# All of x ahead of the rank-16 tables, and unit 0's split weights parked in HBM for unit 8, in a one-core stack of four conditioned residual layers

## The reference, cut to what matters

```python
x = x + einsum('bct,bcd->bdt', x, w0[ia]) + bias[ia][:, :, None]       # layer 0, 64x64 per sample
gate = x @ Wg + (x @ Ag[ia]) @ Bg[ia]                                  # layer 1, 512 -> 2048, rank 16
up   = x @ Wu + (x @ Au[ia]) @ Bu[ia]
h    = silu(gate) * up
x = x + h @ Wd + (h @ Ad[ia]) @ Bd[ia]                                 # 2048 -> 512
x = x + x @ W.T + scal[ib] * (x @ A[ib].T) @ Bm[ib].T                  # layer 2, 512 -> 512, rank 16
x = x + einsum('bct,bcd->bdt', x, w3[ic])                              # layer 3, 64x64 per sample
```

## Time and profile before

| | |
|---|---|
| median of 3 runs | 761.57 us (761.23 to 762.88) |
| the profiled execution | 756.74 us |
| its span, first to last instruction | 754.9 us |
| PE busy | 719.9 us |
| VectorE busy | 583.3 us |
| ScalarE busy | 286.8 us |
| GpSimd busy | 261.7 us |
| mean granted clock of PE | 0.993 |

### The profile page before, as it was taken

One profiled execution on the slowest core, in us unless ns is written; L12 is line 12 of the kernel. 1 busy time (PEld: TensorE's weight loads), 2 busy tenths in 40 slices (PEclk: granted clock), 3 DMA queues, 4 the chain that ended last, 5 costly groups with the idle time before them and its releaser, 6 DMA issues.

```text
span 754.9 us, 10625 instructions
## 1 busy us (share of the span) xinstructions
PE 719.9 (95%) x3666; PEld 610.6 (81%) x3666; DVE 583.3 (77%) x979; ACT 286.8 (38%) x502; POOL 261.7 (35%) x489
## 2 busy tenths in 40 slices
PE   8598889999999999998899999999999999899997
PEld 7576678888888888877778888888888888788885
DVE  5966868797878788789988879797978796864542
ACT  1445423333424243343353433333424242434444
POOL 3933641415233232342237161616253331222100
PEclk9799999999999999999999999999999999999999
DMA  6486321213212121413712222322222043201112
GB/s 155 141 140 201 116 74 35 99 45 103 82 58 84 56 84 56 84 29 112 246 61 94 68 93 70 105 65 88 81 66 85 29 131 93 83 29 51 63 56 83
DMA packets 80725, 66.02 MB, mean 87 GB/s; under 512 B 42912, under 2 KB 65440, under 8 KB 80672
## 3 DMA queue, kind: packets, MB, share of 16 engines
q1 hardware_dynamic: 73056, 45.92, 20.7%
q0 software_dynamic: 7296, 19.41, 8.4%
q10 hardware_dynamic: 320, 0.02, 0.0%
HBM read 56.94 MB, written 8.39 MB: 87 GB/s over the span
## 4 chain that ended last, share of the span: by engine, by line
PE 79%; DVE 9%; issue 6%; DMA 2%; ACT 2%; POOL 1%; SPq 0%; POOLq 0%; DVEq 0%; ACTq 0%
PE bank L1394 34%; PE bank L1494 21%; PE bank L1402 7%; PE bank L1634 5%; PE bank L1504 4%; PE bank L1623 2%; PE bank L1651 2%; DMA BR<-in_L_cond_Bu_dram,boffs 1%; PE bank L1610 1%; PE bank L1640 1%; PE bank L1347 1%; DMA adsel<-in_L_cond_weights_dram 1%; DVE hid L1040 1%; DVE hs L1046 1%; PE bank L1371 1%
## 5 line engine op out<-in xcount | busy, mean ns | idle before, releaser
L1394 PE MATMUL bank<-XC,WC 128*128 128x512 f32 x1344 | 331.8, 393 | 10.6 <-DVE tmp L1014 3.7
L1394 PEld LDWEIGHTS bank<-XC,WC 128*128 128x128 f32 x1344 | 244.0, 189 | 58.2 <-DVE tmp L1014 4.1
L1494 PE MATMUL bank<-hs,wds 128*128 128x512 f32 x768 | 186.3, 391 | 8.0 <-DVE wds L999 4.1
L1494 PEld LDWEIGHTS bank<-hs,wds 128*128 128x128 f32 x768 | 141.8, 188 | 37.2 <-DVE wds L999 4.6
L421 POOL DMA_INDIRECT BR<-in_L_cond_Bu_dram,boffs x64 | 70.7, 1104 | 258.6 <-DVE BL L993 244.0
L421 POOL DMA_INDIRECT BR<-in_L_cond_Bg_dram,boffs x64 | 76.1, 1189 | 92.7 <-DVE BL L993 77.0
L638 ACT ACTIVATE hs<-hid 128x512 fp32r<-128x512 f32 x64 | 40.3, 630 | 168.1 <-DVE hid L1040 112.9
L1057 DVE TENSOR_TENSOR XA<-bank,XA 128x512 f32<-128x512 f32 x128 | 86.4, 686 | 18.4 <-PE bank L1494 14.8
L632 ACT ACTIVATE hid<-hid 128x512 f32<-128x512 f32 x48 | 30.4, 633 | 152.1 <-issue 60.4
L1402 PEld LDWEIGHTS bank<-UT,BL 128*128 128x128 f32 x512 | 76.4, 189 | 10.8 <-issue 2.1
L1402 PE MATMUL bank<-UT,BL 128*128 128x256 f32 x512 | 81.8, 282 | 1.6 <-DVE hid L1037 1.3
(11 more groups left out here) (164 smaller groups left out, 809.5 us busy)
## 6 DMA issues: line engine op xcount, KB each, us to landing
RW<-in_L_cond_Wg_dram SPq DMA_DIRECT2D x16, 512.0 KB
RW<-in_L_cond_Wu_dram SPq DMA_DIRECT2D x16, 512.0 KB
RD<-in_L_cond_Wd_dram SPq DMA_DIRECT2D x16, 512.0 KB
out_dram<-XB SPq DMA_DIRECT2D x16, 256.0 KB, 2.1
XB<-in_x_dram SPq DMA_DIRECT2D x8, 256.0 KB, 7.3
x1park<-XB SPq DMA_DIRECT2D x8, 256.0 KB
x2park<-XA SPq DMA_DIRECT2D x8, 256.0 KB, 2.7
XA<-x1park SPq DMA_DIRECT2D x4, 512.0 KB
```

Of the source, the lines that this page charges most:

```text
L1394: last = nc.tensor.matmul(psum[:, :], WC[:, t, left, a, k, :], XC[:, right, b, k, :], start=(first and k == 0 and n == 0), stop=(k == 1 an ...
L1494: last = nc.tensor.matmul(psD[j % 2][:, :], by_feature(wds[:, f, a, :])[:, j % KT, :], hs[:, f, b, j // KT * 512:(j // KT + 1) * 512], sta ...
```

## The change

1. **x ahead of A.** SyncE's queue loads all first-half pairs and four of the second half before Ag and Au; the other four follow before the table of indices and Wu. GpSimd places the `w0` tiles of pairs 8 to 13 before it selects A, and those of 14 and 15 after. Layer 0 uses three PSUM banks instead of four, so that each `layer0(p)` waits for the copy of p - 3; the bank that is set free holds the second half of `adapters_in`'s result (`u_bank`).
2. **New orders up to unit 1.** All four engines get another list for the start: on PE pairs 8 and 9 go ahead of the first product, 10 and 11 behind it, and `adapters_in` comes after the second and the third product. `us` moves to the part of `WC` where unit 0's up sums will lie, `raw_high(U, 0)` no longer waits for the selects, `sums_high(U, 0)` does. In unit 1 `sum_u3` and `sum_half22` go ahead of `sums_low(U)`, and in units 1 and 9 the `evict`s of tiles 2 to 4 go ahead of an `hs_low`.
3. **Unit 0's split weights kept for unit 8.** `wpark` in HBM takes the finished `WC` of gate and up after unit 0's splits (`weights_out`, 128 x 14,336 bytes each), and unit 1's `raw_high` waits for these stores. At the change of halves they come back (`weights_back`, and `sums_back` for the part of up that `us` covers until the last select). `combine`, `raw_high`, `raw_low`, `sums_high` and `sums_low` of unit 8 are gone for both matrices, and so are the loads of Wg and Wu for unit 8.
4. **New order at the change of halves.** The sums T2 and T1 of the second half are made in units 3 and 4, into `w0second` and `udp`, instead of in unit 7 in place in `XB`. `wd_high` and `wd_low` of units 7 and 15 move up between the last `evict`s, and `xc_low(1, T3)` moves from the end of unit 7's up window to behind the last `hs_low`. The stores of the second half's x1 move behind unit 0's weight stores and the load of unit 2's Wg.

```diff
+    wpark = nc.dram_tensor("wpark", (2, P, 7 * 2 * 2 * P), f32).ap()
...
-            return (psD[0], psD[1], psR[0], psR[1])[p % 4]
+            return (psD[0], psD[1], psR[0])[p % 3]
+        def u_bank(h, m):
+            return (psE, (psR[1], psC)[h])[m % 2]
...
-        us = [wcu[:, t * 1024:(t + 1) * 1024].rearrange("p (a t) -> p a t", a=2) for t in range(2)]
+        us = [wcu[:, 1536 + t * 1024:1536 + (t + 1) * 1024].rearrange("p (a t) -> p a t", a=2) for t in range(2)]
...
-                  {B11: XB11, B21: XB21, B22: XB22, T1: XB12, T2: XB11, T3: XB12, T4: XB21}]
+                  {B11: XB11, B21: XB21, B22: XB22, T1: udp[:, :].rearrange("p (k t) -> p k t", k=2),
+                   T2: w0second[:, :, :].rearrange("p a d -> p (a d)").rearrange("p (k t) -> p k t", k=2),
+                   T3: XB12, T4: XB21}]
...
+        def made(unit):
+            return unit + 1 - (unit >= UNITS)
...
+                def weights_out(t):
...
+                    sp.wait_ge(s_wl[t], 1)
+                    sp.dma_start(wpark[t, :, :], WC[:, t, :, :, :, :].rearrange("p s a k f -> p (s a k f)").bitcast(f32)).then_inc(s_wout[t], 16)
...
+                def weights_back(t):
+                    sp.wait_ge(s_wout[t], 16)
+                    wct = WC[:, t, :, :, :, :].rearrange("p s a k f -> p (s a k f)").bitcast(f32)
+                    if t == G:
+                        sp.wait_ge(s_prod, 8 * nG(0, UNITS - 1) + 8)
+                        sp.dma_start(wct, wpark[t, :, :]).then_inc(s_wback[t], 16)
+                    else:
+                        sp.wait_ge(s_prod, 8 * nP(0, UNITS - 1) + 8)
+                        sp.dma_start(wct[:, 0:1536], wpark[t, :, 0:1536]).then_inc(s_wback[t], 16)
+                def sums_back():
+                    sp.wait_ge(s_sel, 4 * HALVES)
+                    wct = WC[:, U, :, :, :, :].rearrange("p s a k f -> p (s a k f)").bitcast(f32)
+                    sp.dma_start(wct[:, 1536:], wpark[U, :, 1536:]).then_inc(s_wsback, 16)
...
-                for p in range(3, 6):
+                for p in range(3, HP):
                     load_x(p)
+                for p in range(HP, HP + XIN):
+                    load_xin(p)
                 load_a(0)
-                load_x(6)
-                load_x(7)
-                for p in range(HP, HP + XIN):
+                for p in range(HP + XIN, PAIRS):
                     load_xin(p)
                 load_idx(2, idx_c)
                 load_u(0)
                 load_g(1)
-                load_xin(HP + 4)
-                load_xin(HP + 5)
...
-                        load_xin(HP + 6)
-                    if n == 3:
-                        load_xin(HP + 7)
+                weights_out(G)
                 load_d(0)
-                for p in range(HP, PAIRS):
-                    park_x1(p)
                 load_u(1)
+                weights_out(U)
                 for unit in range(ALL):
                     turn = unit == UNITS - 1
                     if unit and unit != UNITS:
@@ -347,16 +376,21 @@
                         load_u(unit + 1)
                     if turn:
                         load_a(1)
-                        load_u(unit + 1)
+                        weights_back(G)
+                        weights_back(U)
                         park_x2()
                         load_d(unit + 1)
-                    if unit + 2 < ALL:
+                    if unit + 2 < ALL and unit + 2 != UNITS:
                         load_g(unit + 2)
+                    if unit == 0:
+                        for p in range(HP, PAIRS):
+                            park_x1(p)
                     if turn:
+                        sums_back()
                         x1_back()
-                sp.wait_ge(s_wl[G], ALL)
-                sp.wait_ge(s_wl[U], ALL)
+                sp.wait_ge(s_wl[G], made(ALL - 1))
...
-                    select_a(0, q, cols)
-                for g in range(2, 4):
-                    late = adapters(8 * g, 8)
-                    for p in range(4 * g, 4 * g + 4):
-                        place_w0(p, late[2 * (p - 4 * g):2 * (p - 4 * g) + 2])
+                late = adapters(16, 8)
+                for p in range(HP, HP + 4):
+                    place_w0(p, late[2 * (p - HP):2 * (p - HP) + 2])
+                late += adapters(24, 8)
+                for p in range(HP + 4, PAIRS):
+                    if p == PAIRS - 2:
+                        for q in range(HQ):
+                            select_a(0, q, cols)
+                    place_w0(p, late[2 * (p - HP):2 * (p - HP) + 2])
                 pool.wait_ge(s_boffs, 1)
...
                     if n_before is not None:
                         act.wait_ge(s_prod, 8 * n_before + 8)
+                    if w == 1:
+                        act.wait_ge(s_wout[t], 16)
                     raw = RW[:, t, :, :]
                     nc.scalar.activation(WC[:, t, A11:A12 + 1, 0, :, :],
...
                     sum_u2(n)
                     if i:
...
+                        raw_low(U, unit)
+                    if unit == 1:
+                        sum_u3(n)
+                        sum_half22(n, tmp[:, 3, :], 1)
+                    if unit != UNITS:
+                        sums_low(U, unit)
                     if i:
                         ad_low(unit - 1)
-                    sum_u3(n)
-                    sum_half22(n, tmp[:, 3, :], 1)
+                    if unit != 1:
+                        sum_u3(n)
+                        sum_half22(n, tmp[:, 3, :], 1)
                     evicts(unit, slots[0], 0)
...
-                    hs_low(unit, 0, 0, 1)
+                    if len(slots[2]) < 2:
+                        hs_low(unit, 0, 0, 1)
                     evicts(unit, slots[2], 0)
+                    if len(slots[2]) == 2:
+                        hs_low(unit, 0, 0, 1)
                     evicts(unit, slots[2], 1)
...
+                    if i == UNITS - 1:
+                        wd_low(unit, 0)
                     evicts(unit, slots[3], 1)
-                    if turn:
-                        xc_low(1, T3)
+                    if i == UNITS - 1:
+                        wd_low(unit, 1)
                     if unit + 1 < ALL and not turn:
                         b_low(2 * unit + 2, 0)
                     hs_low(unit, 1, 1, 3)
                     if unit == 2:
                         t3_sum(1)
                         offsets(1, 2)
-                    if turn:
+                    if unit == 3:
+                        t2_sum(1)
+                    if unit == 4:
                         t1_sum(1)
                     if unit == ALL - 2:
...
-                def first_gate_products(unit):
+                def first_gate_products():
+                    pe.wait_ge(s_xcl, filled(0, B11))
+                    pe.wait_ge(s_wr[G], 1)
+                    p1_product(0, G)
+                    layer0(HP + 2)
+                    layer0(HP + 3)
+                    pe.wait_ge(s_wl[G], 1)
+                    pe.wait_ge(s_xcl, filled(0, T2))
+                    p6_product(0, G)
+                    adapters_in(0, 0)
+                    layer0(HP + 4)
+                    layer0(HP + 5)
+                    pe.wait_ge(s_xcl, filled(0, T1))
+                    p5_product(0, G)
+                    adapters_in(0, 1)
+                    select(0, 0)
+                    select(0, 1)
+                    layer0(HP + 6)
+                    layer0(HP + 7)
+                def second_half_products(unit):
                     h, n = unit // UNITS, 2 * unit
-                    if h:
-                        pe.wait_ge(s_xcl, filled(h, B11))
-                        pe.wait_ge(s_wr[G], unit + 1)
-                        select(h, 0)
-                        p1_product(n, G)
-                        select(h, 1)
-                    pe.wait_ge(s_wl[G], unit + 1)
+                    pe.wait_ge(s_xcl, filled(h, B11))
...
+                    if n == 0:
+                        pe.wait_ge(s_um, 1)
+                        select(0, 2)
+                        select(0, 3)
```

More of the change, by code:

```diff
@@ L641, in gate_window @@
                     n, i = 2 * unit, unit % UNITS
-                    p1_copy(n)
+                    if unit:
+                        p1_copy(n)
                     if i:
@@ L720, in _ @@
                         xc_high(1, T1)
-                        raw_high(G, unit + 1, 2 * unit, s_gld)
                         u_high(1, 0)
-                        sums_high(G, unit + 1)
                         xc_high(1, T4)
@@ L979, in g_combine @@
                 def g_combine(unit):
-                    combine(G, unit, (s_gld, 16 * (unit + 1)))
+                    combine(G, unit, s_gld)
                 def p_combine(unit):
-                    combine(U, unit, (s_uld, 16 * (unit + 1)))
+                    combine(U, unit, s_uld)
                 def a_low(h, q):
@@ L1164, in _ @@
                 layer3_zeros()
+                biases(1)
+                move_matrices()
```

(12 more changed lines are left out.)

157 lines of the change are left out of this document (78 added, 79 removed).

## The result

The changed kernel takes 751.96 us (median of 4 executions, 750.89 to 753.36) against 761.4 us (755.76 to 762.88), a ratio of 0.9893 with a 95% interval of 0.9856 to 0.993. Timed once more, beside the experiments, it is 752.54 against 758.67 us, 0.9923 (0.9894 to 0.9952). So it is faster by 6 to 9 us. The two profiled executions differ by less, 756.74 and 752.52 us; the experiments show part of why.

A forecast was written before the change was run, and what follows sets the result against it. PE, busy 719.9 us (95% of the span), was taken as the bound, so only its idle and slow time could be had. 2.8 + 3.9 + 3.1 + 0.1 = 9.9 us off the median of 761.57 gave 751.7, range 746.5 to 757.5.

The forecast's parts named there:

- Start, up to the gather: Kernel start: gather_b(1) would start 2.8 us earlier than 60.19, at 57.4; bounds 2.8 and 5.4.
- I take no change: Gather of Bu in unit 0: its 6.03 us latency stays despite the wpark stores; bounds 2 us less, 6 more.
- Rival 1: Stores to wpark hold up the gathers at 55 to 75 us, costing 3 to 5 us: 755 to 757; chance 0.18.
- Unit 1: PE's waits in unit 1: 1.7 us less for sum_u3 and 2.20 for an evict gone, together 3.9.
- The change of halves: Unit 7 to unit 8: shorter PE waits there and in unit 8 gain 3.1 us; bounds 1.4 and 4.5.
- the first 1.4 us: After unit 7's last product: of PE's 3.58 us of waits for wd_low and an evict, 1.4 would be saved.
- the 1.6 in unit 8: Unit 8: earlier sum_u2 and sum_u3 save 0.38 and 0.85 us, earlier b_low and ud_mask 0.4 more.
- rival 3: Change of halves gains only 1.4 us, as the last 1 MB or unit 8's gather is late: 753.5; chance 0.12.
- Rival 4: ScalarE stops at raw_high(G, 1) until gate's store lands; kernel slower, 767 if at 84 us; chance 0.05.
- The end: Unit 15: PE's wait of 1.1 us for wd_low goes, but the evict behind keeps its time: 0.1 us gained.

The follow-up runs named there:

- units 1 and 9 as before: The changed kernel with units 1 and 9 in their old order (sum_u3 behind sums_low and ad_low, evicts behind the hs_low): 757.23 us, ratio 0.9979.
- T3 is later: The changed kernel with the low part of T3 moved behind the second evict of unit 7, from ahead of the first: 749.17 us, ratio 0.9879.
- again: The changed kernel itself, unaltered, timed and profiled once more beside the experiments: 752.54 us.
- shorter rows: The changed kernel with wpark laid out so that a transfer's row is 2,048 bytes long instead of 14,336: 750.69 us, ratio 0.99.
- without the parking: The changed kernel with unit 8's weights loaded and split again, nothing stored to or read from wpark: 746.64 us, ratio 0.9838.
- up's store later: The changed kernel with the store of up's split weights held until unit 0's gather of Bu has landed: 750.17 us, ratio 0.9889.

## Why the prediction was right, and where it was wrong

751.7 was forecast and 751.96 measured, but the number is luck: two errors cancel. The sum of 9.9 us was too large against the profiled execution from which it was worked out (it gave 4.2 there), and the median of 761.57 from which I took it off was 3 to 4 us above what 69 later executions of the kernel before give (median 757.9).

- **Start, up to the gather.** 2.8 forecast, 4.1 measured (56.05). The selection of A ended at 35.75 (36.0 forecast), though not in the way told: it began at 23.3, since the tables for `w0` were there 3.9 us earlier, and took 12.47 us instead of 6.75. T2's low part, PE's product at 33 (34) and the slow `adapters_in` (4.04 us, 4.1 told) came as forecast; part of the 4.1 is the earlier start of layer 0 (8.4 us), which in the profiles of before and of its variants varies from 8.6 to 10.6.
- **"I take no change" for the gather's 6.03.** The step that failed. It took a latency under traffic for the gather's own. It lands in 3.6 us without the stores, in 7.4 with them. So the start was worth 2.0 at its end, and 5.3 without the stores. Rival 1 had the mechanism, with its price of 3 to 5 us (3.3 measured), but as a loss against 6.0; the cause it named, long rows, is refuted.
- **Unit 1.** 3.9 forecast, 4.2 measured in the profile, the wait at 0.80 and none for an `evict`, as told. What was missed: in many executions the same waits also let the clock fall. That costs 1.5 us more where it happens once (43.9 against 42.4 us) and 4.3 where it happens twice (46.7), and it can be why the medians differ by more than the profiles.
- **The change of halves.** 3.1 forecast; in the profile 1.8 were lost. Of the first 1.4 us 0.9 were there: on PE it is 57.0 us from unit 7's milestone to unit 8's first product where the clock stays up (units 1 and 9 as before), against 57.9 before. The wait for the `evict` was 1.88 (2.1 told), but the one for `ad_low` 0.71 (0.3 told), so 1.0 of the 3.58 us of idle time had gone, not 1.4; the two waits as told would themselves have left 1.2. And I priced the new waits as idle time only. And of the 1.6 in unit 8 nothing came: `sum_u2` and `sum_u3` were early as told, but the gather for unit 8 landed in 6.2 us, VectorE stood 3.01 us for it with `sum_c12` behind it, and PE waited 0.49 and 0.88 us further on, which took back what had gone of the waits for the two sums. That is rival 3's mechanism.
- **Rival 4** (ScalarE stops at `raw_high(G, 1)`) did not come; no wait of PE for returning weights either. **The end**: 0.1 forecast, 0.2 lost; the `wd_low` wait went and 1.00 for `ad_low` came.
- **Parking as a whole** was counted as a gain of some 1.6 us. It is a loss of 5.9, or of 4.4 once T3 is later.

Open: where 2.6 of these 5.9 us lie, and when the clock falls. With the same wait of 1.88 us at the change of halves it fell in four profiled executions (changed, again, shorter rows, without the parking) and not in two (up's store later, units 1 and 9 as before).

## What to carry to other kernels

A wait of PE is priced twice: its idle time, and the slower work behind it when the clock falls; an idle stretch of 2 us in a busy kernel is worth removing even if one profile shows no slow stretch behind it. The latency of a small gather in a profile is not its own, so look what stands ahead of it and beside it on the queues: here 3.6 us beside one load of 0.5 MB, 7.4 with two stores of 1.8 MB around it. Saving VectorE's work by moving megabytes lost 6 us where VectorE had time to spare. Choose a milestone on the engine that bounds the kernel: ScalarE's `silu` in unit 8 moved by 0.7 us where PE did not. Take a base from many executions: three of them were 3.7 us off, as much as a whole term of the sum.

## What the runs showed of the hardware

- Of the 69 executions of the kernel before, 22 had a mean granted clock under 0.987 and a median of 761.5 us, 37 had 0.990 or more and 756.8. The spread is 8.6 us in all, and these two medians are 4.7 apart, so more than half of it goes with the clock. In the two profiles where unit 1 showed a slow stretch the idle time ahead was the same 2.5 us as in the one that showed none.
- GpSimd's 16 copies for A took 12.47 us at 23 to 36 us and 6.75 before. VectorE was busy throughout in most of that time (2.00 of 2.00 in each slice from 24 to 32 of the changed kernel run again), but that alone does not explain it: from 20 to 28 us, where the same copies ran in the kernel before, VectorE was busy for 7.66 of 8.00 us. The cause is open.
- A row of 34 dummy 128 x 128 matmuls of one constant operand took 4.01 us, 0.12 each; at the program's start 24 of them took 5.38, 0.22 each, though the profile shows a granted clock of 1.00 in both places.
- The changed kernel's stores to `wpark` move in pieces of 14,336 bytes, half of which took 0.54 us or less each, and the gather of Bu in 128 pieces of 4,096 bytes. With pieces of 2,048 bytes in the stores the gather was as late.
